# Last layer of a two-layer gated transformer stack: projections and attention as one program of slots, with scores and weighted sums on row and column groups of TensorE

## The reference, cut to what matters

```python
s_std = jnp.sqrt(jnp.clip(w_std, 1e-08, None))
s_rec = jnp.sqrt(jnp.clip(w_rec, 1e-08, None))
Wb = Wa * col_scale[None, :]          # s_std, s_rec by head; 1 for V
fused = x @ Wb                        # 512 -> q, k (24 of 32 wide), v, and the last 8 of q and k
q_tail = jnp.where(use_ra, K_low, Q_low)
k_tail = jnp.where(use_ra, Q_low, K_low)
scores = jnp.einsum('bhtd,bhsd->bhts', Qf, Kf) * scale
scores = jnp.where(causal[None, None], scores, jnp.finfo(scores.dtype).min)
attn = jax.nn.softmax(scores, axis=-1)
out = jnp.einsum('bhts,bhsd->bhtd', attn, V)
return y @ Wp
# and around it:
x = x + jnp.tanh(g_ffn[1]) * _L1_ffn_ref(_layernorm(x, axis=-1), L1_ffn_Wa, L1_ffn_Wp, L1_ffn_w_std, L1_ffn_w_rec)
```

## Time and profile before

| | |
|---|---|
| Runs of the kernel before | 2279.47, 2278.62, 2275.20 us; median 2278.62 us |
| The profiled execution | 2281.86 us, of which the span from first to last instruction is 2280.1 us |
| Mean granted TensorE clock | 0.967 of 2.4 GHz |
| Busy share of the span | PE 94%, DVE 57%, ACT 53%, POOL 30% |
| Last block (both programs) | from 1917.66 us to the end of the span: 362.4 us |
| Its first matmul of a projection block | at 1944.47 us |
| Its first scores | at 2088.84 us |

### The profile page before, as it was taken

The page is one execution under the profiler, slowest core; times in us unless marked ns, Lnnn a source line. Parts: engine busy times, 40 slices in busy tenths (PEclk is TensorE's granted clock), DMA queues, the critical chain, the costliest instruction groups (busy, mean ns, idle before and its releaser), DMA issues. The chain is left out here.

```text
span 2280.1 us, 38223 instructions
## 1 busy us (share of the span) xinstructions
PE 2133.8 (94%) x12952; PEld 1760.1 (77%) x12952; DVE 1294.6 (57%) x2455; ACT 1202.5 (53%) x3080; POOL 686.0 (30%) x812
## 2 busy tenths in 40 slices
PE   6999999999999999999969995999999995897998
PEld 4777777777767888898858884888888884786887
DVE  4555555555544343564345555777777775315897
ACT  4666666666653333353323335667766663114785
POOL 1423523424321000000004443555555553002442
PEclk9999999999999999999979997999999998898899
DMA  5433535525238010100033343322223212100111
GB/s 145 128 109 117 151 88 162 155 81 174 80 111 276 9 56 1 65 1 28 1 113 113 110 124 123 104 95 94 71 99 102 94 59 80 43 7 27 33 48 41
DMA packets 161350, 200.50 MB, mean 88 GB/s; under 512 B 63280, under 2 KB 101168, under 8 KB 160720
## 3 DMA queue, kind: packets, MB, share of 16 engines
q1 hardware_dynamic: 161232, 198.91, 27.7%
HBM read 124.99 MB, written 73.89 MB: 87 GB/s over the span
## 5 line engine op out<-in xcount | busy, mean ns | idle before, releaser
L1629 POOL TENSOR_TENSOR c_probs<-c_probs,c_rsum 112x375 f32<-112x375 f32 x256 | 213.0, 835 | 231.2 <-DVE c_rsum L1739 225.3
L1735 DVE TENSOR_REDUCE c_nmax<-c_score 112x1 f32<-112x375 f32 x256 | 136.2, 533 | 97.4 <-PE c_score L1805 97.4
L536 ACT ACTIVATE a_probs<-a_score,a_nmax 112x375 f32<-112x375 f32 x256 | 144.2, 572 | 59.7 <-DVE a_nmax L690 59.7
L1156 ACT ACTIVATE b_silu<-b_gate,b_ug_scale 128x512 f32<-128x512 f32 (+1 forms) x64 | 40.7, 635 | 250.7 <-PE b_up L1230 250.6
L1683 ACT ACTIVATE c_pT_hi<-c_turned 125x336 fp32r<-125x336 f32 x256 | 115.6, 452 | 107.9 <-PE c_turned L1813 107.8
L543 ACT ACTIVATE a_pT<-a_turned 125x672 f32<-125x672 f32 x128 | 93.7, 732 | 135.2 <-PE a_turned L878 135.2
L1185 DVE SCALAR_TENSOR_TENSOR b_hidden<-b_up,b_ug_scale,b_silu 128x512 f32<-128x512 f32 (+1 forms) x64 | 43.7, 683 | 213.3 <-ACT b_silu L1156 213.3
L1354 POOL TENSOR_TENSOR q_x_ve<-q_x_mv,keep_ln_eps 128x1 f32<-128x1 f32 x14 | 2.7, 190 | 488.1 <-DVE q_x_mv L1431 488.1
L1676 ACT ACTIVATE c_probs<-c_score,c_nmax 112x375 f32<-112x375 f32 x256 | 148.2, 579 | 0.0
L847 PE MATMUL a_shared<-a_w_lo,a_kT_hi 128*125 128x512 f32 x384 | 135.2, 433 | 0.0
L1813 PEld LDWEIGHTS c_turned<-keep_ident,c_probs 112*125 112x125 f32 x768 | 121.7, 189 | 15.9 <-POOL c_probs L1629 7.1
(11 more groups left out here) (281 smaller groups left out, 6007.2 us busy)
## 6 DMA issues: line engine op xcount, KB each, us to landing
q<-q_qT SPq DMA_DIRECT2D x14, 1024.0 KB
c_q_raw<-q SPq DMA_DIRECT2D x16, 896.0 KB
k<-ab_stage SPq DMA_DIRECT2D x16, 752.0 KB, 4.1
c_k_raw<-k SPq DMA_DIRECT2D x16, 752.0 KB
v<-ab_stage SPq DMA_DIRECT2D x48, 250.0 KB
c_v_raw<-v SPq DMA_DIRECT2D x16, 750.0 KB
ab_lead<-in_ctx_dram SPq DMA_DIRECT2D x16, 672.0 KB
wug<-a_ug_turned SPq DMA_DIRECT2D x32, 256.0 KB, 3.8
```

The costliest lines, as they stand in the source:

```text
L536: last = act.activation(probs[:, n % 2, i, :], score[0:S, i, 0:T], ACT.Exp, bias=nmax[:, b % 2, h:h + 1], accum_out=sums[:, b % 2, h:h + 1])
L1629: pool.tensor_tensor(probs[:, h % AHEAD, :], probs[:, h % AHEAD, :], rsum[:, p, h:h + 1].broadcast_to([S, T]), ALU.mult).then_inc(scaled, 1)
L1735: dve.tensor_reduce(nmax[:, p, h:h + 1], score[h % AHEAD][0:S, 0:T], axis=AX.X, op=ALU.max, negate=True).then_inc(max_done, 1)
```

## The change

The two programs become one, `phase_d`, with the loops written out. There are 64 slots (a sequence and a group of four heads), and most have an *item* beside their attention work: one block of q, k or v, or one or two chunks of the turned x, for the next group of four sequences. START and LATER say which item stands in which slot; 11 items stand ahead of slot 0. All items but the first 11 go through one bank, `work`.

In a slot t PE does: scores of slot t+2 for heads 0 and 1; the weighted sum of slot t-1; scores of slot t+2 for heads 2 and 3; the items; every fourth slot the output projection; and last the turning of slot t's probabilities. Scores take q and k of each head from its own 32 partitions (row groups), two heads at once into two banks, with N = 112. The weighted sum has v as the stationary side and writes each head's transposed output to its own 32 partitions (column groups), so that the output needs no turning. POOL divides the probabilities by their sums before they are turned. The block-diagonal key matrix, its splits on POOL, the memsets, `e_q`, `e_k`, `e_v`, `d_on` and `turn_out` go. ACT makes every hi part, DVE every lo part straight out of the bank (v has no lo part).

Scaling and reordering of Wa moves into `phase_b`, to its steps 7, 9, 11 and 13, with four loads and four stores, and the last stage loads the ordered weights from HBM, block by block. SP waits there for each chunk to be done before it enters the loop over the tiles of `phase_b`.

```diff
 def phase_b(nc, keep, io, ab):
+    ORDER = {7: 0, 9: 1, 11: 2, 13: 3}
...
         @block.sync
+            for c in range(DC):
+                if c:
+                    sp.wait_ge(wa_done, 2 * c)
+                    store_ordered(c - 1)
+                sp.dma_start(wa_raw, io["Wa"].rearrange("(c p) n -> c p n", p=P)[c, :, :]).then_inc(wa_loaded, 16)
+            sp.wait_ge(wa_done, 2 * DC)
+            store_ordered(DC - 1)
             for g in range(GROUPS):
...
         @block.vector
+                if t == LATE + 2:
+                    clip_scales()
+                if t in ORDER:
+                    order_weights(ORDER[t])
...
 def phase_d(nc, keep, io):
+    SETS, RING = 2, 3
+    SLOTS = B * G
+    weights = ("q0", "k0", "q1", "k1", "v", "q2", "k2", "q3", "k3", "p")
+    START = {-1: "x0 x1 x2 x3 q0 k0 q1 k1 v0 q2 k2", 0: "q3 k3", 1: "v1", 2: "v2", 3: "v3"}
+    FIRST_SCORES = {"q1": (0, 0), "k1": (0, 1), "v0": (1, 0), "q2": (1, 1)}
+    LATER = {4: "x0 x1", 5: "x2 x3", 6: "q0", 7: "k0", 8: "q1", 9: "k1", 10: "v0", 11: "q2", 12: "k2", 13: "q3", 14: "k3",
+             15: "v1", 16: "v2", 18: "v3"}
...
         @block.sync
+            for b in range(BPG):
+                load_normal(b)
+            for name in weights:
+                load_weight(name)
...
         @block.gpsimd
+            for t in range(SLOTS):
+                r = t % RING
+                pool.wait_ge(rsum_done, t + 1)
+                pool.tensor_tensor(probs[:, r, :, :], probs[:, r, :, :], rsum[:, r, :].unsqueeze(2).broadcast_to([S, HPG, S]),
+                                   ALU.mult).then_inc(scaled, 1)
...
         @block.scalar
+            for t in range(SLOTS + 2):
+                b, i = divmod(t, G)
+                if i == 1 and b:
+                    out_hi(b - 1)
+                if t + 1 < SLOTS:
+                    exps(t + 1)
+                for g, name in items(t):
+                    item_hi(g, name)
+                if t == 1:
+                    weights_hi("p")
...
         @block.vector
+            def item_lo(g, name):
+                if name[0] == "v":
+                    return
+                src, n = bank(g, name), int(name[1])
+                dve.wait_ge(work_hi, number(g, name))
...
+            for t in range(SLOTS + 3):
+                b, i = divmod(t, G)
+                if i == 1 and b:
+                    out_lo(b - 1)
+                if i == 2 and b:
+                    finish(b - 1)
+                if t + 2 < SLOTS:
+                    maximum(t + 2)
+                if t + 1 < SLOTS:
+                    reciprocal(t + 1)
+                for g, name in items(t):
+                    item_lo(g, name)
+                if t == 1:
+                    weights_lo("p")
+                if t < SLOTS:
+                    probs_copy(t)
+                if t % 16 < BPG and t // 16 + 1 < NG:
+                    normalize(BPG * (t // 16 + 1) + t % 16)
...
         @block.tensor
+            def free_bank(g, name):
+                n = number(g, name) - 1
+                used = n - 4 if n < FIRST else n - 1
+                if used >= 0:
+                    pe.wait_ge(work_hi, used + 1)
+                    pe.wait_ge(work_lo, split_number(*order[used]))
...
+            def scores(t, half):
+                b, i = divmod(t, G)
+                g, j = divmod(b, BPG)
+                if half == 0:
+                    if t >= SETS:
+                        pe.wait_ge(probs_ready, t - SETS + 1)
+                    pe.wait_ge(work_lo, max(split_number(g, f"q{i}"), split_number(g, f"k{i}")))
+                else:
+                    pe.wait_ge(first_pair, t + 1)
                 for n, (s, r) in enumerate(PASSES):
+                    for a in range(2):
+                        part = rows(2 * half + a)
+                        last = pe.matmul(score[0:S, SETS * (t % SETS) + a, half * S:(half + 1) * S],
+                                         q[s][part, g % 2, i, j * S:(j + 1) * S], k[r][part, g % 2, i, j * S:(j + 1) * S],
+                                         start=n == 0, stop=n == len(PASSES) - 1)
+                last.then_inc(scores_ready if half else first_pair, 1)
...
+            def weigh(t):
+                b, i = divmod(t, G)
+                g, j = divmod(b, BPG)
+                pe.wait_ge(pT_copied, t + 1)
+                if i == 0:
+                    pe.wait_ge(work_hi, number(g, f"v{j}"))
+                    if b:
+                        pe.wait_ge(o_split, b)
+                for n in range(HPG):
+                    h = HPG * i + n
+                    last = pe.matmul(outp[rows(n), i * S:(i + 1) * S], v[:, g % 2, j, h * HD:(h + 1) * HD], pT[:, t % 2, n, :],
                                      start=True, stop=True)
...
+            for t in range(SLOTS + 2):
+                b, i = divmod(t, G)
+                if t + 2 < SLOTS:
+                    scores(t + 2, 0)
+                if 0 < t <= SLOTS:
+                    weigh(t - 1)
+                if t + 2 < SLOTS:
+                    scores(t + 2, 1)
+                for g, name in items(t):
+                    run_item(g, name)
+                if i == 1 and b:
+                    project(b - 1)
+                if t < SLOTS:
+                    turn(t)
```

More of the change, by code:

```diff
@@ new lines, in items, with number, split_number, rows @@
+    def items(t):
+        found = [(0, name) for name in START.get(t, "").split()]
+        for g in range(1, NG):
+            found += [(g, name) for name in LATER.get(t - 16 * (g - 1), "").split()]
+        return found
+    order = [item for t in range(-1, SLOTS) for item in items(t)]
+    FIRST = len(items(-1))
+    def number(g, name):
+        return order.index((g, name)) + 1
+    def split_number(g, name):
+        return sum(what[0] != "v" for _, what in order[:number(g, name)])
+    def rows(j):
+        return slice(HD * j, HD * j + HD)
@@ L2150, in keys_lo @@
-        def keys_lo(eng, signal, b, p, j):
-            eng.wait_ge(k_hi, HPG * b + j + 1)
-            r = slice(HD * j, HD * j + HD)
-            eng.tensor_tensor(k[1][r, p, :, j, :], qkv["k"][r, :, bass.ds(b * S, S)], f32(k[0][r, p, :, j, :]), ALU.subtract).then_inc(signal, 1)
+        score = m.ps("score", [P, 2 * SETS, 512])
+        work, tail, turned, outp = (m.ps(n, [P, 512]) for n in ("work", "tail", "turned", "outp"))
+        w_loaded = {name: m.sem(f"w_loaded_{name}") for name in weights}
@@ new lines, in phase_d, with bank, weight_of @@
+        rsum_done, scaled, turned_ready, pT_copied = (m.sem(n) for n in ("rsum_done", "scaled", "turned_ready", "pT_copied"))
+        out_ready, o_hi, o_split, y_ready, x_done = (m.sem(n) for n in ("out_ready", "o_hi", "o_split", "y_ready", "x_done"))
+        block = m.block()
+        def bank(g, name):
+            n = number(g, name) - 1
+            return (work, tail, turned, outp)[n % 4] if n < FIRST else work
+        def weight_of(name):
+            n = int(name[1]) + (G if name[0] == "k" else 0)
+            return slice(n * P, (n + 1) * P)
@@ L2162, in body, with load_normal @@
[L2162 to L2170 removed]
+            def load_normal(b):
+                if b >= BPG:
+                    sp.wait_ge(work_ready, number(b // BPG - 1, "x3"))
+                sp.dma_start(xn[:, b % BPG, :], io["x3"][b, :, :]).then_inc(xn_loaded[b % BPG], 16)
@@ L2171, in _ @@
+            for b in range(2):
+                load_residual(b)
+            for b in range(BPG, 2 * BPG):
+                load_normal(b)
+            for b in range(B):
+                store(b)
+                if b + 2 < B:
+                    load_residual(b + 2)
+                if b % BPG == 1 and b // BPG + 2 < NG:
+                    for n in range(BPG):
+                        load_normal((b // BPG + 2) * BPG + n)
             for p in range(2):
-                sp.wait_ge(x_stored[p], 16 * (B // 2) + 16)
+                sp.wait_ge(x_stored[p], 16 * (B // 2))
@@ new lines, in exps @@
+            def exps(t):
+                act.wait_ge(max_done, t + 1)
+                if t >= RING:
+                    act.wait_ge(turned_ready, t - RING + 1)
+                for j in range(HPG):
+                    half, a = divmod(j, 2)
+                    last = act.activation(probs[:, t % RING, j, :], score[0:S, SETS * (t % SETS) + a, half * S:(half + 1) * S], ACT.Exp,
+                                          bias=nmax[:, t % RING, 2 * a + half:2 * a + half + 1], accum_out=sums[:, t % RING, j:j + 1])
+                last.then_inc(probs_ready, 1)
```

654 lines of the change are left out of this document (244 added, 410 removed).

## The result

The changed kernel takes **2331.3 us** (median of 4 runs, 2329.6 to 2337.6), the kernel before 2277.5 beside it: ratio 1.0242, 95% interval 1.022 to 1.0263. It is slower by 54 us; 2315 had been predicted. Its profiled execution has a span of 2329.7 us (before 2280.1) and a mean granted clock of 0.959 (before 0.967).

A forecast was written before the change was run, and what follows sets the result against it. PE bounds both long stretches. Slot 0 at 1957.6 plus 336.9 of slots, 10.2 of end and +12 half clock gave span 2316.7, forecast 2315 us; range 2265 to 2345, likeliest case 2295 to 2335.

The forecast's parts named there:

- One slot: Last block's slots, set by instruction order on DVE and PE: q or k 5.27 us, v 4.85, empty 2.95.
- Extras: Additions to attention slots: 0.55 us a sequence for the output's lo part ahead of the next sum, 0.5 a group for normalisation.
- Sixteen slots: Last block, one group of four sequences: 88.8 us, where before it was 75.2.
- Scores on row groups: Scores in each slot: 0.44 us a half, both halves 0.88 against 0.68 before; row groups save nothing.
- Weighted sum: Sum in each slot, with column groups: 8 matmuls take 0.30 us against 0.81 before.
- The start: Start of last block: PE's first block at 1931.4 instead of 1944.5, 13 us earlier; slot 0 begins at 1957.6.
- Ordering in `phase_b`: Wa's ordering, four times 2.1 us, fits DVE's waits in `phase_b` and costs nothing; rival, not hidden: +8, 2323, chance 0.03.
- The end: After slot 64 begins: last sum, splits, last projection and store take 10.2 us.
- The half clock: Slots where PE has little to do: seven projections or blocks at 4.4 against 2.8 us, +12 (bounds 0 and 40).
- the half clock stays: Rival, on PE's clock: a third of the blocks run at 4.4 us, another +33, 2348; chance 0.12.
- Shorter waits: Rival, in slots: splits and copy hide behind turning and scores, slot 3.96 us, total 2257; chance 0.16 with 2265 to 2275 between.
- On row groups the stream alone counts: Rival, in scores: 0.26 us for 0.44 in each slot, -12, 2303, still slower; chance 0.05.

The follow-up runs named there:

- the first four experiments: Changed kernel with: turning ahead of items, 2340.1 us; copy ahead of the last item's lo part, 2318.3; both moves, 2298.65; both plus all scores ahead of the sum, 2289.5.
- the kernel with four fillers: Changed kernel plus four 512-column matmuls, results unread, ahead of the weighted sum in most slots (every fourth left out): 2318.0 us, ratio 1.0173.

## Why the prediction was right, and where its sum was off

The sign, the range and the mechanism held; the likeliest case was given as 2295 to 2335 and holds the 2331. The span was to be 2316.7 and is 2329.7. By its steps:

- **One slot.** q or k 5.27 predicted, 5.28 to 5.32 measured at full clock; v 4.85 and 4.90 (the terms given for it add up to 4.89); empty 2.95 (2.99 by its terms) and 2.81. PE is idle before the sum and DVE's copy releases it, as the text said. That it is the order of instructions and no engine's work is what the first four experiments show: the same operations in another order take 46 us less in the loop.
- **Extras.** Predicted +0.55 a sequence for the output's lo part, in a q or k slot 5.90 against 5.29, +0.6, in a v slot 5.99 against 4.90, +1.1. The step was right as to what it costs a q or k slot; with the two other waits gone it was worth 1.0 in each slot that had it.
- **Sixteen slots.** 88.8 predicted. Added up from slots at full clock it is 89.6. The trace has those with x chunks, and q or k with a projection, only with some half clock; they are taken from the kernel with four fillers (5.88 and 7.35), and the x slot with a projection, 8.88 even there, is put at 7.7, an estimate.
- **Scores on row groups.** 0.44 a half predicted. Starts of passes 0.10 apart, 0.43 from the first pair to the item in the slot shown. The rule of the Trainium skill (TensorE: Matmul & The Clock Gate, Part 3) that I weighed against it is given for 512 columns; on 112 no gain shows. Both halves take about as long as I forecast, 0.88 us where the products of 448 columns took 0.68.
- **Weighted sum.** 0.30 predicted, 0.33 up to the next line (2099.98 to 2100.31), for 0.81 before. The column groups do overlap: in the trace four of the eight matmuls start within 0.03 us and the other four 0.12 us later, where before they started one by one, 0.10 apart.
- **The start.** First block predicted at 1931.4, measured at 1925.3. Of the 6.1 us, 3.6 are the stages ahead (above), and 2.5 come because x is normalised sooner: the old stage loaded head scales first, and I had taken its 1926.59 over as the time of the first turned x; it is 1920.53 now. From there to the first block it is 4.7, as forecast. The first sum comes at 1959.3 where 1957.6 + 9.3 = 1966.9 was forecast, 7.6 us earlier.
- **Ordering in `phase_b`** costs nothing: 9.0 us less idle time there, in the operation that the orderings stand beside, and the stage is no longer.
- **The end.** 10.2 predicted, 10.4 measured.
- **The half clock is the term that failed.** "I count seven projections or blocks at half clock, 4.4 against 2.8, so +12 (bounds 0 and 40)." In the loop 12 of the 15 projections have part of their slot at half clock, and with x chunks, empty slots and some blocks it is 105.8 us. The stretches cost 98.0 + 95.7 + 98.5 - 3 x 89.6 = 23.4 in the three groups, 47.0 - 39.3 = 7.7 in the slots without items, and about 2 at the beginning: 33 us. The kernel with fillers says 34, by a way that is nearly independent (two of its slot lengths are in the 89.6). So -7.6 (start) + 21 (clock) and less than 1 for all the rest make the 13 us between 2316.7 and 2329.7. That the rest is so small is partly luck: slots 4 to 50 come out 3.1 us longer than forecast and those from 51 on 3.6 shorter (slots 62 and 63, which have no scores to make, take 1.64 where 2.95 was put down). And 3.6 of the 7.6 belong to the stages ahead in this one profiled execution; between medians, 2315 and 2331.3, the prediction was 16 too low.

The rival that the half clock stays (2348, +33 beyond the 12) was nearer in its mechanism than I gave it credit for: 21 of its 33 us came. "Shorter waits" needed a copy that lands within 0.8 us of the item's end; it landed about 1.9 us behind it (the turning that follows the item starts at 2103.29, the copy ends at 2105.22) and only the experiments made it land sooner. "On row groups the stream alone counts" is out: a pass costs 0.10, not 0.05.

Where the gain went: the change does take away the 9.8 us between the programs and 15.6 at the start. It gives back 14.4 us with every group of four sequences by waits in a chain across three engines, and about 33 by the clock, of which some 10 were there before as well (an estimate: 0.33 to 0.4 of the 27.3 us at half clock in the earlier trace rows).

## What to carry to other kernels

When an item of one chain is put into the slot of another, look on every engine for what stands behind it in program order: here one copy stood behind a subtraction that it has nothing to do with, and a move on each of two engines made the kernel 33 us faster, while of the two alone one made it 9 slower and the other 13 faster. A wait in a tight loop can be paid twice: once as idle time, and again when the granted clock falls, so cost both, and count the time at half clock over the whole loop, not only over its long products. Splitting a matrix of few columns over row groups saved nothing here; over column groups of the output it took the weighted sum from 0.81 to 0.33 us.

## What was not expected of the hardware

- **Added work made the kernel faster.** 8 matmuls between x chunks and 3 in empty slots, 512 columns each: 2272.8 to 2261.9 us, granted clock in the loop 0.91 to 0.98. Each microsecond at half clock was worth about 0.33 of the loop in the kernel with fillers; in the one with doubled scores, 14 us for 34, 0.4.
- **The clock falls where no wait is long.** In the changed kernel PE is never idle for more than 1.63 us at a time between 2060 and 2250, and is busy for 84%, and yet the granted clock falls there again and again. The stretch from 2111.22 on begins right behind the longest of these waits:

```profile
2094.71:2111.22 16.51, 12.87 (x112) 10.62 (x115) 8.56 (x17) 6.09 (x28) 2.80 (x3) 1.00 0.10 29
2111.22:2120.11 8.89, 8.61 (x52) 6.92 (x54) 2.68 (x6) 1.89 (x9) 0.93 (x1) 0.81 0.00 0
```

  Waits aren't needed for it either. In the kernel with the output's split moved PE is idle for 0.3 us in the 7.0 ahead of the stretch below, a v slot and an empty one, and the clock falls at the turning and the x chunks that follow:

```profile
2047.89:2054.90 7.01, 6.70 (x70) 4.68 (x68) 4.86 (x10) 2.88 (x15) 1.74 (x2) 1.00 0.22 68
2054.90:2068.55 13.65, 10.75 (x60) 8.15 (x53) 7.07 (x14) 5.82 (x25) 1.99 (x3) 0.50 0.00 0
```

  Whether waits or stretches of short matmuls bring it about was not separated: the fillers fill both.
- **The same instructions meet either clock.** In the changed kernel the slot of v1 takes 6.45 us, part of it at half clock, in slot 15, and 4.88 at full clock in slot 31, both behind a wait of 1.01 us. In the kernel with one chunk a slot, slots 18 to 21 take 17.6 us, 13.7 of them at half clock, and slots 34 to 37, the same work, 12.3 at full clock. So the time at half clock can be forecast as a range, and not slot by slot.
- **A score pass takes 0.10 us at full clock, and 0.19 at half**, so its limit runs with TensorE's clock.

```profile
2198.55 0.39 PE L2282 MATMUL f_score<-f_k_lo,f_q_hi 32*112 32x112 f32 x2
2198.74 0.38 PE L2282 MATMUL f_score<-f_k_hi,f_q_lo 32*112 32x112 f32 x2
2198.93 0.38 PE L2282 MATMUL f_score<-f_k_hi,f_q_hi 32*112 32x112 f32 x2
```
